# Mamba mixing matrix from two stacked products instead of twelve small ones, in a fused decoder kernel

## What is computed

```python
xz = layernorm(x) @ W_in.T                 # 512 -> 2 * 1024
x_proj, z = split(xz)
x_conv = silu(conv_b + causal_conv4(x_proj, conv_w))
Bm, Cm, dt = split(x_conv @ W_xproj.T)     # 16, 16, 1 columns
dt = clip(softplus(dt), 0.001, 0.1)
def step(h, t):                            # h: 1024 channels x 16 states
    A_bar = exp(clip(dt[t] * A, -20, 0))
    B_bar = clip(dt[t] * Bm[t], -10, 10)
    h = clip(A_bar * h + B_bar * x_conv[t], -100, 100)
    return h, h @ Cm[t]
y = scan(step) * silu(z) + x_conv * D
x = x + y @ W_out.T
```

## Time and profile before

| | us |
|---|---|
| median of 3 runs | 2684.91 (2684.54 to 2685.75) |
| the profiled execution, its own time | 2681.22 |
| its span in the profile | 2679.5 |
| PE busy in the span | 2466.5 |
| VectorE busy | 1545.8 |
| ScalarE busy | 1215.0 |

### The profile page before, as it was taken

The page is one execution under the profiler, slowest core; times in us unless marked ns, Lnnn a source line. Parts: engine busy times, 40 slices in busy tenths (PEclk is TensorE's granted clock), DMA queues, the critical chain, the costliest instruction groups (busy, mean ns, idle before and its releaser), DMA issues. The chain is left out here.

```text
span 2679.5 us, 48118 instructions
## 1 busy us (share of the span) xinstructions
PE 2466.5 (92%) x17244; PEld 2184.7 (82%) x17245; DVE 1545.8 (58%) x2561; ACT 1215.0 (45%) x1912; POOL 647.4 (24%) x1040
## 2 busy tenths in 40 slices
PE   5999999999999699999999995289999999999997
PEld 5999999999998587878778773178889888888886
DVE  5788788788787366666656554733343343433432
ACT  6465565565564344444444432034443434434442
POOL 3111121121122444444435332010220203113021
PEclk9899999999999899999999996589999999999998
DMA  3010100110113656666665642132342424334231
GB/s 113 33 34 25 40 33 25 39 33 25 38 36 97 178 164 174 173 177 178 173 176 158 180 117 98 36 94 71 105 117 84 106 94 106 94 107 106 66 80 20
DMA packets 232738, 254.72 MB, mean 95 GB/s; under 512 B 68264, under 2 KB 158376, under 8 KB 232464
## 3 DMA queue, kind: packets, MB, share of 16 engines
q1 hardware_dynamic: 191504, 231.17, 29.0%
q0 software_dynamic: 40960, 20.41, 4.4%
HBM read 182.47 MB, written 68.80 MB: 94 GB/s over the span
## 5 line engine op out<-in xcount | busy, mean ns | idle before, releaser
L2199 DVE TENSOR_TENSOR d_h_l<-d_hf,d_h_h 128x616 fp32r<-128x616 f32 x124 | 99.1, 799 | 394.2 <-ACT d_h_h L2025 394.2
L401 PE MATMUL a_psP<-s_xnT_h,s_w_l 128*128 128x256 f32 x1024 | 307.9, 301 | 15.4 <-ACT a_zs L641 9.6
L1938 PE MATMUL d_psH<-d_xgT_h,d_w_l 128*128 128x308 f32 x1024 | 315.4, 308 | 3.2 <-ACT d_hf L2061 1.8
L1939 PE MATMUL d_psH<-d_xgT_l,d_w_h 128*128 128x308 f32 x1024 | 312.3, 305 | 0.0
L1940 PE MATMUL d_psH<-d_xgT_h,d_w_h 128*128 128x308 f32 x1024 | 312.1, 305 | 0.0
L2061 ACT ACTIVATE d_hf<-d_psH,d_b1c 128x308 f32<-128x308 f32 x256 | 130.6, 517 | 383.8 <-PE d_psH L1940 381.3
L402 PE MATMUL a_psP<-s_xnT_l,s_w_h 128*128 128x256 f32 x1024 | 299.5, 292 | 0.0
L403 PE MATMUL a_psP<-s_xnT_h,s_w_h 128*128 128x256 f32 x1024 | 298.9, 292 | 0.0
L1902 POOL DMA_INDIRECT out_dram<-d_ob,d_to x40 | 103.7, 2592 | 686.0 <-ACT d_ob L2078 676.0
L1938 PE MATMUL d_psO<-d_w_h,d_h_l 128*123 128x512 f32 x620 | 244.2, 394 | 0.0
L1939 PE MATMUL d_psO<-d_w_l,d_h_h 128*123 128x512 f32 x620 | 244.0, 394 | 0.0
(11 more groups left out here) (367 smaller groups left out, 6189.8 us busy)
## 6 DMA issues: line engine op xcount, KB each, us to landing
d_w<-in_W_dram SPq DMA_DIRECT2D x64, 1024.0 KB, 5.6
b_qst<-qs_d SPq DMA_DIRECT2D x48, 512.0 KB, 6.6
b_kst<-ks_d SPq DMA_DIRECT2D x48, 512.0 KB, 6.5
s_raw<-in_x_dram SPq DMA_DIRECT2D x16, 512.0 KB, 3.6
s_xres<-in_x_dram SPq DMA_DIRECT2D x16, 512.0 KB, 3.6
x_d<-s_xres SPq DMA_DIRECT2D x16, 512.0 KB, 2.8
s_raw<-in_ctxT_dram SPq DMA_DIRECT2D x16, 512.0 KB, 10.3
s_xres<-x_d SPq DMA_DIRECT2D x16, 512.0 KB, 9.3
```

Of the source, the lines that this page charges most:

```text
L401: pe.matmul(out, lo_w, hi_x, start=first, stop=False)
L1938: pe.matmul(out, lo_w, hi_x, start=first, stop=False)
L1939: pe.matmul(out, hi_w, lo_x, start=False, stop=False)
L2199: dve.tensor_tensor(out, a, b_, ALU.subtract).then_inc(done, 1)
```

## The change

EB becomes 128 x 256 and EC 128 x 256: the 16 states of block i lie on partitions 16 i to 16 i + 15, and the contraction runs over all 128. EC is made zero outside a block's own 32 tokens, by a 0/1 pattern `mine` on the C rows, so that one product with all blocks gives each target token its own block's reference. Two matmuls give the whole of M: 128 x 256 and, for the source tokens 128 to 255, 128 x 128.

To have the rows on all 128 partitions, B, C and lam now lie in one tile `rows` (16 x 769), and SP copies it eight times, 16 partitions each, to `every` (128 x 769). EB and EC are then made at 128 x 256 with a per-partition reference `ref`: a masked copy, a reduction over 8 elements, and two subtractions with a bound.

The last part of `rows_2` moves from d = 4 to d = 5, the exponentials from d = 5 to d = 6, `rows_3` from d = 6 to d = 7. POOL makes `mine` at the start, three instructions. Three semaphores that only mark a passed wait become one.

```diff
@@ SP
+                if cur:
+                    wait(sp, rows_c, 2 * b)
+                    sp.sem_inc(passed_s, 1)
+                    sp.wait_ge(rows_b, 12 * b + 5)
+                    for i in range(NB):
+                        sp.dma_start(every[i * N:(i + 1) * N, :], rows[:]).then_inc(every_ld, 16)
@@ POOL, at the start
+            g.memset(mine[:], 1.0).then_inc(setup_pool, 1)
+            (two affine_select on mine, 128 x 256)
@@ PE
-                    for n in range(NI):
-                        i = n if n < NB else n - NB + HB
-                        c = i * BL if n < NB else S + (n - NB) * BL
-                        mm = pe.matmul(psX[:, c:c + BL], EB[:, n, :], EC[:, i * BL:(i + 1) * BL], start=True, stop=True)
+                    pe.matmul(psX[:, 0:S], EB[:, 0:P], EC[:], start=True, stop=True)
+                    mm = pe.matmul(psX[:, S:S + P], EB[:, P:], EC[:, P:], start=True, stop=True)
                     mm.then_inc(m_mm, 1)
@@ ACT
-                    if cur and d == 5:
-                        act.wait_ge(rows_b, 11 * b + 11)
+                    if cur and d == 6:
+                        act.wait_ge(rows_b, 12 * b + 12)
                         act.activation(abar[:], l_r[:], ACT.Exp).then_inc(exps_b, 1)
                         act.activation(EB[:], EB[:], ACT.Exp, scale=-1.0).then_inc(exps_b, 1)
                         act.activation(EC[:], EC[:], ACT.Exp).then_inc(exps_b, 1)
@@ DVE rows_1
+                    wait(dve, every_ld, 16 * NB * b)
@@ DVE rows_2, part 1 (d = 3)
-                        (EB 16 x 1024 and 16 x 512 from lam and the references)
+                        ch.did(dve.tensor_tensor(rng[:], before[:, :, 0], ends[:, :, BL - 1], ALU.subtract))
+                        ch.did(dve.scalar_tensor_tensor(out=ab[:], in0=Bb, scalar=-1.0, in1=Bb, op0=ALU.mult, op1=ALU.max))
@@ DVE rows_2, part 2 (d = 4 before, d = 5 after)
-                        (EC, rng, ab, then the floor under EB, 16 x 1536)
+                        dve.wait_ge(every_ld, 16 * NB * b + 16 * NB)
+                        if first:
+                            dve.wait_ge(setup_pool, 11)
+                        sums = every[:, 2 * S:]
+                        ch.did(dve.tensor_tensor(refm[:], sums[:, 0:S].rearrange("p (i t) -> p i t", t=BL)[:, :, 0], mine[:, :, 0], ALU.mult))
+                        ch.did(dve.tensor_tensor(every[:, S:2 * S], every[:, S:2 * S], mine[:].rearrange("p i t -> p (i t)"), ALU.mult))
+                        ch.wait()
+                        ch.did(dve.tensor_reduce(ref[:], refm[:], AX.X, ALU.add))
+                        ch.wait()
+                        ch.did(dve.tensor_scalar(EB[:], sums[:, 1:], ref[:, 0:1], -60.0, ALU.subtract, ALU.max))
+                        ch.did(dve.tensor_scalar(EC[:], sums[:, 1:], ref[:, 0:1], 0.0, ALU.subtract, ALU.min))
@@ DVE rows_3 (d = 6 before, d = 7 after)
-                    (EB times B at 16 x 1024 and 16 x 512, EC times C at 16 x 256)
+                    dve.tensor_tensor(EB[:], EB[:], every[:, 0:S], ALU.mult).then_inc(rows_c, 1)
+                    dve.tensor_tensor(EC[:], EC[:], every[:, S:2 * S], ALU.mult).then_inc(rows_c, 1)
```

More of the change, by code:

```diff
@@ L90, in mamba_phase @@
     NB = S // BL
-    HB = P // BL
-    NI = NB + NB - HB
+    assert NB * N == P
     CL = 8
@@ L123, in mamba_phase @@
         y2_h, y2_l = sb("y2_h", [P, 2, S], F32R), sb("y2_l", [P, 2, S], F32R)
-        dt_r, l_r, Bb, Cr, ab = (sb(n, [N, S]) for n in ("dt_r", "l_r", "Bb", "Cr", "ab"))
+        dt_r, l_r, ab = (sb(n, [N, S]) for n in ("dt_r", "l_r", "ab"))
+        rows, every = sb("rows", [N, 3 * S + 1]), sb("every", [P, 3 * S + 1])
+        Bb, Cr, lam = rows[:, 0:S], rows[:, S:2 * S], rows[:, 2 * S:]
+        mine, refm, ref = sb("mine", [P, NB, BL]), sb("refm", [P, NB]), sb("ref", [P, 1])
         gb = l_r
         abar = sb("abar", [N, S])
-        lam = sb("lam", [N, S + 1])
-        EB, EC = sb("EB", [N, NI, P]), sb("EC", [N, S])
+        EB, EC = sb("EB", [P, S]), sb("EC", [P, S])
         rng, scl = sb("rng", [N, NB]), sb("scl", [N, 2])
@@ L289, in _ @@
                             pattern=[[1, P]], channel_multiplier=-1).then_inc(setup_pool, 1)
+            g.memset(mine[:], 1.0).then_inc(setup_pool, 1)
+            pool.wait_ge(setup_pool, 9)
+            g.affine_select(out=mine[:], in_=mine[:], compare_op=ALU.is_ge, fill=0.0, base=0,
+                            pattern=[[-N, NB], [0, BL]], channel_multiplier=1).then_inc(setup_pool, 1)
+            pool.wait_ge(setup_pool, 10)
+            g.affine_select(out=mine[:], in_=mine[:], compare_op=ALU.is_ge, fill=0.0, base=N - 1,
+                            pattern=[[N, NB], [0, BL]], channel_multiplier=-1).then_inc(setup_pool, 1)
             def rsqrt(b):
@@ L343, in flags @@
                 with pool.If(beyond > 999):
-                    for r, row in enumerate((abar, Bb, Cr)):
-                        pool.dma_start(rows_dram[r], row[:]).then_inc(fb_dma, 16)
+                    for r, row in enumerate((abar[:], Bb, Cr)):
+                        pool.dma_start(rows_dram[r], row).then_inc(fb_dma, 16)
                     pool.wait_ge(fb_dma, 48)
@@ L672, in _ @@
             dve.memset(ones_row[:], 1.0).then_inc(setup_dve, 1)
-            dve.memset(lam[:, 0:1], 0.0).then_inc(setup_act, 1)
+            dve.memset(rows[:, 2 * S:2 * S + 1], 0.0).then_inc(setup_act, 1)
             dve.memset(fl[:], 0.0).then_inc(setup_act, 1)
@@ L776, in rows_2 @@
                         ch.wait()
[L777 to L780, removed]
+                        before = lam[:, 0:S].rearrange("n (i t) -> n i t", t=BL)
@@ L781, in rows_2 @@
+                        ends = lam[:, 1:S + 1].rearrange("n (i t) -> n i t", t=BL)
+                        ch.did(dve.tensor_tensor(rng[:], before[:, :, 0], ends[:, :, BL - 1], ALU.subtract))
+                        ch.did(dve.scalar_tensor_tensor(out=ab[:], in0=Bb, scalar=-1.0, in1=Bb, op0=ALU.mult, op1=ALU.max))
                     else:
                         ch.n = 7
-                        ch.did(dve.tensor_tensor(EC[:].rearrange("n (i t) -> n i t", t=BL), ends,
-                                                 ref[:, :, 0:1].broadcast_to([N, NB, BL]), ALU.subtract))
@@ L855, in body @@
                             bounds(0)
-                        if d in (2, 3, 4):
-                            rows_2(d - 2)
+                        if d in (2, 3, 5):
+                            rows_2(d // 2 if d > 3 else d - 2)
                         if d >= 2 and d % 2 == 0:
@@ L2302, in block_kernel @@
     y = out.rearrange("b s d -> (b s) d")
-    passed_v, passed_s, passed_p = (nc.alloc_semaphore(n) for n in ("passed_v", "passed_s", "passed_p"))
+    passed_v = passed_s = passed_p = nc.alloc_semaphore("passed")
     T = n_tok // P
```

24 lines of the change are left out of this document (7 added, 17 removed).

## The result

| | before | after |
|---|---|---|
| median, us | 2685.33 (2684.54 to 2686.17, 4 runs) | 2634.51 (2634.01 to 2637.70, 4 runs) |
| the profiled execution, its own time | 2681.22 | 2637.70 |
| its span | 2679.5 | 2636.1 |

The change makes the kernel 1.8% faster: ratio 0.9816, 95% interval 0.9801 to 0.9832. After's is the slowest of its four runs and before's 3.7 us under the median of its own shown ahead, so 7.3 us of the medians' difference lie outside the account. Beside the later experiments the kernel before has medians of 2683.0 and 2682.5, some 2.5 us lower.

A forecast was written before the change was run, and what follows sets the result against it. PE was taken to set the Mamba pace; 21 (shorter passes) + 10.5 (clock) + 3.3 (first product's pass) = 35 us off 2681.2 gave 2646, predicted as a 2650 median, range 2640 to 2667.

The forecast's parts named there:

- attention: The attention passes behind the Mamba phase: the sum held no term for them, so no gain or loss.
- batch 1: First pass with a product, at the low clock: 3.8 us gained, about 0.5 lost in pass 0, 3.3 left.
- The 3.7 us added: The runs' median lay 3.7 us above the profiled execution, so 2646 became 2650 for the median.
- The 14 equal passes: Mamba passes from batch 2 to 16: 1.5 us shorter each, 21 us, plus 10.5 us from the clock; all about 48.2.
- The product and the next wait: PE's product takes 0.75 us, then 0.7 waiting for xnT_l; `in_proj(0)` starts 1.3 us earlier, DVE's line 722 1.5 earlier.
- The clock: The slow stretch behind the 24 small matmuls stays away: 11 passes at 0.95 us, 10.5 us gained.
- Rival 1: The slow-clock stretch behind the product stays: gain 24.5 us, time 2660; chance 0.17.
- DVE, ACT and the transfers: Per Mamba pass, DVE sheds 5.5 us and adds 2.2, ACT's line 628 falls; all hidden under PE, no gain by itself.
- Just in time: At d = 5, the eight row transfers take 7.5 us of the 7.8 between SP's release and DVE's use.
- Rivals 2 and 3: Steps d = 5 to 7: delayed exponentials, time 2665, chance 0.09; late transfers, up to 2731, chance of cost to PE 0.08.
- The 0.5: In pass 0, `rows_2` and the exponentials in a row with `moments` lose about 0.5 us.
- The free time behind the transfers: 1.7 us free between `normalize` and the transpose needing it; PE notices only DVE waits for `every` beyond that.

The follow-up runs named there:

- a_order: The kernel after the change, with both halves of the transpose moved ahead of PE's last output product; median 2626.33 us, ratio 0.9791.
- a_narrow: The kernel after, with its product cut into twelve matmuls of 32 columns again, over 128 contraction rows; median 2670.94 us, ratio 0.9954.
- b_wide: The kernel before, with only its product made two wide matmuls over 16 rows, leaving out references (another M); median 2634.36 us, ratio 0.9818.
- b_pad: The kernel before, with 16 semaphore increments that nobody waits on ahead of PE's first wait; median 2671.42 us, ratio 0.9953.
- a_twice: The kernel after, with eight more transfers of the same rows, to memory, ahead of its own in each pass; median 2642.66 us, ratio 0.9858.

## Why the prediction was right, and where it was wrong

The steps that failed are two terms of the sum: attention, put at nothing because the sum ended with the Mamba phase, gave 9.3 us, and batch 1, put at 3.3, gave 7.15. The 3.7 us added to come from the profiled execution to the median failed too: after's median lies 3.2 below its profiled execution. The 14 equal passes, the greater part of the sum, came out as worked.

**The product and the next wait: right.** Priced 0.75 us, it takes 0.81; PE's wait for xnT_l, priced 0.7, is 0.85 in this pass and 0.8 in the mean; the start of `in_proj(0)` was to move by 1.3 us and moved by 1.1, DVE's mask product by 1.5 and moved by 1.45. The period was to be 48.2 and is 48.20. That the pass shrinks by DVE's 1.5 and not by PE's 1.1 is as the prediction had it, since `x_dbl` follows the convolution; the table under a_order shows it over five kernels.

**The clock: right, for a reason that was only half of it.** The falls are gone in all 14 passes. The prediction put them down to small matmuls. By a_narrow short matmuls alone do not bring them, by b_wide 16 rows alone do not; they came with both together. The change removed both, so a reason that was half right gave the right number, which is luck. Rival 1 did not happen. PE had no idle time ahead of the falls, and with the new wait of 0.8 us a pass there are none. The Trainium skill's page "TensorE: Matmul & The Clock Gate" (section "Why this matters for your kernels") ties a fall in mid-kernel to PE idling between bursts of matmuls. The falls here came without idle time and went when some was added, so that rule does not cover them, and the measurement decides.

**DVE, ACT and the transfers: right that they cost and give nothing in the 14 equal passes.** There b_wide is as fast without any of it (48.13 us for 48.20). The groups of after, passes 2 to 15 (busy, mean ns, idle before):

```profile
L805 DVE TENSOR_TENSOR a_every<-a_every,a_mine 128x256 f32<-128x256 f32 x14 | 5.9, 419 | 0.0
...
L814 DVE TENSOR_TENSOR a_EB<-a_EB,a_every 128x256 f32<-128x256 f32 x14 | 5.9, 418 | 0.0
```

```profile
L645 ACT ACTIVATE a_EB<-a_EB 128x256 f32<-128x256 f32 x14 | 5.6, 400 | 0.0
```

The masked copy and a product take 0.42 us for the 0.41 priced from line 797, ACT's exponential 0.40 for 0.42. The eight transfers: issue time (ns min/median/max), then the median us to landing:

```profile
L271 SPq DMA_DIRECT2D a_every<-a_rows x128: 526/589/1756, 52.7 to 776.7; - x128
```

```profile
a_every<-a_rows SPq DMA_DIRECT2D x128, 48.1 KB, 2.2
```

The median issue is the 0.59 taken from the earlier trace rows, and the landing 2.2 us, under the 2.8 of the nearest row. DVE is never shown waiting for `every`. "Just in time" was right: the last of the eight landed 0.02 to 1.2 us ahead of DVE's first use in passes 1 to 15, and 0.5 or more in twelve of them, where the working left 0.3. Rivals 2 and 3 did not happen.

**Batch 1: the step that failed in sign and size.** The term was 3.8 - 0.5 = 3.3; the two stretches gave 5.96 + 1.19 = 7.15. The 0.5 was charged for a crowded end of pass 0. The crowding cost nothing: ACT waits 2.37 us for DVE there (its timeline, from 61.3 to 63.68), but its next table load, 1.28 us, already ran ahead of that wait, at 60.02, and the exponential of EB takes 0.40 us for 1.47; and `normalize` comes at 66.62 where it came at 67.69, because 2.3 us of `rows_3` on DVE shrank to 0.8. The size of that gain is uncertain: product 1 starts between 69.84 and 70.63 in the five kernels with before's pass 0, and between 68.78 and 70.05 in the four unpadded ones with after's, 0.7 us earlier in the mean. And the low clock was priced for the product alone, though it lasted to 81.0 us before and only to 71.0 after; that is the 2.4 us that b_wide lacks.

**Attention: the step that was missing.** The sum ended with the Mamba phase, so the range had no term of either sign for what a shorter program does to later code. It measured 9.3 us in the profiled executions, and 11 in b_pad by medians. What the runs showed in its place: attention's pace goes with where its code lies in PE's program, and the change moved it by 240 instructions. The account closes: 34.8 summed up, + 9.3 here, + 3.85 in batch 1, - 0.3 in the fourteen passes, - 4.3 given back, are 43.4. The range, which reached only 10 us below the forecast, shut out the time that came.

**The free time behind the transfers: mis-sized, without effect.** The prediction had 1.7 us from the distance between `normalize` and its transpose; a_twice shows about 2.5.

**Open.** 3.7 us were given back behind the fifteenth logits, in the last attention pass, the routing and the experts, and 0.6 between the last product and the first logits; neither was followed. The stretch behind the fifteenth logits takes 1057 to 1063 us in the ten profiled kernels and does not go with the place of PE's code (b_wide 1058.8, after 1062.4). The 7.3 us between the medians' and the profiles' difference are of the size of the spread of runs (the kernel before spans 2676 to 2690 us beside the experiments).

## What to carry to other kernels

A shortened stage pays up to the next thing its engine waits for: read that wait's own chain first. Then find the event behind which the rest of the pass always takes the same time (here DVE's mask product, 46.8 us) and move that forward, as a_order does; the idle time of the busiest engine alone does not say what can be won. Ask what a stage of many short, low matmuls costs behind itself as well, in the granted clock of the windows that follow it. And when a change adds or removes instructions and the gain in question is under half a per cent, time it once more with a few idle instructions ahead of the program: here 16 of them were worth 11 us, more than a quarter of the whole Mamba gain.

## What the runs showed of the hardware

- Twenty-four float32 instructions of 32 columns over 16 rows were followed by a fall of the clock to 1.2 GHz in 11 of 14 passes; over 128 rows, in none, at the same length (2.76 us for 2.79). Four wide instructions over 16 rows (b_wide) brought none either.
- Sixteen instructions more, or 240 less, ahead in PE's program moved the second of the three 16 KB fetches of a repeated pass from 22 to 33 us to 18 to 20 us behind the logits, and two batches of attention took 89.8 to 90.2 us instead of 91.6 to 92.2.
- In the 15 attention passes with that fetch at 27.9 to 29.6 us, the issue of the second K store took 0.98 us in the mean, up to 1.63, for 0.50 in the 60 passes with the early fetch.
- A semaphore increment on PE took 0.15 us: 240 of them 36.8 us.
- Each transfer of 16 rows of 3076 bytes left 32 packets in the trace, 16 of them of 4 bytes: 236834 packets in the page of after against 232738, 4096 more for 128 transfers, half of them under 512 bytes (70312 - 68264 = 2048).
